# An attention and expert layer on one core: attention passes written out, TensorE order mixed, states as 32x32 diagonal blocks

## What is computed

```python
scores = jnp.einsum('bhid,bhjd->bhij', q, k) * mask      # mask: 0.95**(i-j) for i >= j, else 0
out = jnp.einsum('bhij,bhjd->bhid', scores, v)
out = out.transpose(0, 2, 1, 3).reshape(B, S, D) @ Wo + bo
# group norm of each (batch, head) over its 16 channels and 512 tokens, then gamma and beta
```

## Time and profile before

| | us |
|---|---|
| median of 3 runs | 2576.47 |
| lowest, highest | 2572.44, 2585.91 |
| the profiled execution | 2559.96 |
| its span | 2558.1 |
| PE busy in the span | 2361.7 |
| DVE, ACT, POOL busy | 1349.9, 987.9, 1311.0 |

### The profile page before, as it was taken

How to read it: one execution, slowest core, us unless ns; L and a number is a source line. 1 busy time by engine, 2 the same in 40 slices (tenths; PEclk the granted TensorE clock), 3 DMA queues, 4 the chain that set the end, 5 groups by cost and what they waited for, 6 DMA issues and landing times.

```text
span 2558.1 us, 74894 instructions
## 1 busy us (share of the span) xinstructions
PE 2361.7 (92%) x29260; PEld 2093.5 (82%) x29260; DVE 1349.9 (53%) x2531; ACT 987.9 (39%) x1801; POOL 1311.0 (51%) x2216
## 2 busy tenths in 40 slices
PE   6988888899887899599999999999999999999997
PEld 5777777787766677498999999999999999999996
DVE  2555555566554566595444554445554455544443
ACT  4444444555434454233333333333333333333332
POOL 4333444444333343346666666666666666666453
PEclk9999999999888899699999999999999999999999
DMA  3122222222111211223322323323332323322232
GB/s 118 52 69 72 73 69 76 68 79 75 56 64 51 68 61 60 91 34 49 82 45 46 83 42 49 79 45 49 76 47 46 78 49 64 60 47 45 48 49 25
DMA packets 129237, 155.99 MB, mean 61 GB/s; under 512 B 11008, under 2 KB 118656, under 8 KB 129024
## 3 DMA queue, kind: packets, MB, share of 16 engines
q0 software_dynamic: 49152, 67.14, 16.3%
q1 hardware_dynamic: 79872, 85.58, 10.4%
HBM read 85.57 MB, written 67.11 MB: 60 GB/s over the span
## 4 chain that ended last, share of the span: by engine, by line
PE 56%; POOL 1%; DVE 1%; issue 0%; DMA 0%; ACT 0%; POOLq 0%; DVEq 0%; ACTq 0%
PE hidden L1281 27%; PE y L1296 27%; PE xt L1268 2%; POOL out L1134 0%; POOL xg L1124 0%; DMA out<-y,scatter_idx 0%; DVE best_index L199 0%; DVE g_hi L1248 0%; DVE best L195 0%; DMA xg<-xn_rows,step_idx 0%; DVE g_lo L1250 0%; DVE rows L203 0%; DVE xt_lo L1237 0%; ACT y L1183 0%; ACT g L1197 0%
## 5 line engine op out<-in xcount | busy, mean ns | idle before, releaser
L1134 POOL DMA_INDIRECT out<-y,scatter_idx x256 | 436.8, 1706 | 408.7 <-ACT y L1183 349.2
L1248 DVE CAST g_hi<-g 128x512 fp32r<-128x512 f32 x512 | 281.7, 550 | 673.9 <-ACT g L1197 673.8
L1296 PE MATMUL y<-w_hi,g_hi 128*128 128x256 f32 x2048 | 572.2, 279 | 1.8 <-ACT y L1183 1.8
L1296 PE MATMUL y<-w_lo,g_hi 128*128 128x256 f32 x2048 | 566.6, 277 | 0.0
L1296 PE MATMUL y<-w_hi,g_lo 128*128 128x256 f32 x2048 | 566.5, 277 | 0.0
L1197 ACT ACTIVATE g<-hidden 128x512 f32<-128x512 f32 x512 | 306.6, 599 | 400.5 <-PE hidden L1281 400.5
L1281 PE MATMUL hidden<-xt_hi,w_lo 128*128 128x512 f32 x1024 | 404.4, 395 | 0.0
L1281 PE MATMUL hidden<-xt_lo,w_hi 128*128 128x512 f32 x1024 | 402.2, 393 | 0.0
L1281 PE MATMUL hidden<-xt_hi,w_hi 128*128 128x512 f32 x1024 | 399.0, 390 | 1.5 <-DVE xt_lo L1237 1.5
L1250 DVE TENSOR_TENSOR g_lo<-g,g_hi 128x512 fp32r<-128x512 f32 x512 | 386.0, 754 | 17.7
L1296 PEld LDWEIGHTS y<-w_hi,g_hi 128*128 128x128 f32 x2048 | 384.8, 188 | 2.0 <-ACT y L1183 2.0
(11 more groups left out here) (138 smaller groups left out, 3809.7 us busy)
## 6 DMA issues: line engine op xcount, KB each, us to landing
x<-in_x SPq DMA_DIRECT2D x32, 512.0 KB, 4.8
w_stage<-in_w SPq DMA_DIRECT2D x16, 1024.0 KB, 5.7
xn_rows<-xn SPq DMA_DIRECT2D x32, 512.0 KB, 3.4
res<-in_x SPq DMA_DIRECT2D x32, 512.0 KB, 3.8
out<-res SPq DMA_DIRECT2D x32, 512.0 KB, 3.0
xg<-xn_rows,step_idx POOLq DMA_INDIRECT x256
out<-y,scatter_idx POOLq DMA_INDIRECT x256, 3.9
cst<-in_cst SPq DMA_DIRECT2D x1, 484.0 KB, 4.4
```

What stands on the lines that cost most here:

```text
L1134: pool.indirect_dma_start(out_rows, bass.IndirectOffsetOnAxis(sidx[:, k:k + 1], 0), y[:, k, :], None, compute_op=ALU.add).then_inc(scatter ...
L1248: dve.tensor_copy(g_hi[:, m, :], g32[m % 4][:]).then_inc(gh_ready, 1)
L1296: last = pe.matmul(yb[k % 2][:, 0:D], g_[:, m, cols], w[par][:, m, :], start=i == 0, stop=i == 3 * FT - 1)
```

## The change

1. The two loops of the attention block are gone: `passes` writes out all 35 passes on PE, DVE, ACT, POOL and SP, so all waits have constant values, and `wait_apart` is left out of this block. The loops of the expert block stay.
2. The state stays compact: `states` multiplies the 128x32 blocks with a mask of 32 columns, 448 columns in all where it had 1792. The inter-chunk product is made of four matmuls on 32x32 tiles on the array's diagonal, one for each pair of heads, instead of one on the full array. All four write the same PSUM bank, in different partitions.
3. `values` is cut: `inter` of the first half comes right behind `project`, the products of scores and values are done chunk by chunk (0 to 3), and TensorE's order is mixed anew; `av_done` counts four for each batch.
4. The orders of ACT, DVE and POOL are changed to fit. `rsqrt_steps` takes one step of third order and one of second in place of three of second: 11 chained steps instead of 13 without the eps step (which moved out). POOL's group chain goes from 19 steps to 17.
5. DVE computes the group's moments between the two masks of the first scores, and a whole round of top-k at one place; the softmax steps go to the end of the pass.

```diff
-        def passes(eng, one):
-            for b in range(-2, 2):
-                one(b, b % 2)
-            with eng.Fori(1, MID // 2) as i:
-                one(2 * i, 0)
-                one(2 * i + 1, 1)
...
+        def passes(one):
+            for b in range(-2, B + 1):
                 one(b, b % 2)
...
             def states(f, fp):
...
-                dve.tensor_tensor(tm[fp][:].rearrange("p j h (r x) -> p (j h) r x", r=PAIRS),
-                                  sbk[:, 0, 0:n * 32].rearrange("p (g x) -> p g x", x=32).unsqueeze(2)
-                                  .broadcast_to([P, n, PAIRS, 32]),
...
+                dve.tensor_tensor(tm[fp][:].rearrange("p j h x -> p (j h) x"),
+                                  sbk[:, 0, 0:n * 2 * HD].rearrange("p (g x) -> p g x", x=2 * HD),
+                                  bdm.unsqueeze(1).broadcast_to([P, n, 2 * HD]), ALU.mult).then_inc(tm_ready, 1)
...
+            def inter(b, par, z):
...
                     for h in range(DH):
                         at = h * 256 + c * SUB
-                        pe.matmul(ob[:, s, at:at + SUB], tm[par][:, g - 1, h, :],
-                                  qd[par][:, h, g * SUB:(g + 1) * SUB], start=s not in opened, stop=False,
-                                  skip_group_check=True)
+                        for p in range(PAIRS):
+                            rows = slice(32 * p, 32 * p + 32)
+                            pe.matmul(ob[rows, s, at:at + SUB], tm[par][rows, g - 1, h, :],
+                                      qd[par][rows, h, g * SUB:(g + 1) * SUB], start=g in (1, 2) and h == 0,
+                                      stop=False, skip_group_check=True)
```

More of the change, by code:

```diff
@@ L584, in one @@
                 if has(a):
-                    projected(a, 0)
-                if has(l):
-                    norm(l, par, 0)
-                if has(a):
-                    projected(a, 1)
+                    for h in range(DH):
+                        projected(a, h)
                 if has(f):
@@ L593, in one @@
                 if has(l):
+                    norm(l, par, 0)
+                if has(f):
+                    value(f, 2)
+                if has(l):
                     norm(l, par, 1)
@@ L697, in residual, with softmax, one @@
                                   ALU.add).then_inc(res_ready, 1)
-            def one(b, par, k, group=None):
-                f, fp, a = b + 1, 1 - par, b - 1
-                if has(b + 2):
-                    stats(b + 2, k + 1, par)
-                if isinstance(b, int) and b == -2:
-                    split_weights()
-                if group == 1:
-                    route.as_float(dve, 0)
+            def softmax(b, par):
+                if par and has(b):
+                    for m in range(SOFTMAX_SPLIT):
+                        route.softmax_step(dve, b // 2, m, scored)
+                elif not par and has(b - 1):
+                    for m in range(SOFTMAX_SPLIT, Routing.STEPS):
+                        route.softmax_step(dve, b // 2 - 1, m, scored)
+            def one(b, par):
+                f, fp, a, g = b + 1, 1 - par, b - 1, b - MID
                 if has(a):
@@ L743, in one @@
                         x_split(b + 2, h)
-                if has(f):
-                    states(f, fp)
                 if has(a):
@@ L748, in one @@
                         residual(a, j)
[L749 removed]
+                if has(f):
+                    states(f, fp)
+                if b not in (MID, B):
+                    softmax(b, par)
+                if b == B:
                     for r in range(Routing.LAST_PASS_ROUNDS // 2, Routing.LAST_PASS_ROUNDS):
                         route.whole_round(dve, 1, r)
[L753 to L765 removed]
+            passes(one)
         @block.tensor
@@ L973, in one @@
                         project(b, a, h)
+                if has(b):
+                    inter(b, par, 0)
                 if has(f):
-                    for t in range(TT):
-                        value_gate(b, f, t)
-                if isinstance(b, int) and b == B:
+                    value_gate(b, f, 0)
+                    value_gate(b, f, 1)
+                if b == B:
                     route.turn_top(pe, 0, sbk[:, 0, :])
@@ L995, in one @@
                 if has(f):
-                    running_state(b, f, fp)
-                if has(b):
-                    values(b, par, 1)
-                if has(a):
-                    for j in range(2):
-                        turn_y(b, a, j)
-            passes(pe, one)
+                    running_state(b, f, fp, False)
+                if has(a):
+                    turn_y(b, a, 0)
+                if has(f):
+                    running_state(b, f, fp, True)
+                if has(a):
+                    turn_y(b, a, 1)
+                if has(b):
+                    values(b, par, 3)
+            passes(one)
 def expert_block(nc, xn_d, out, w1, w2, cst, route, s1, w_in, out_stored):
```

287 lines of the change are left out of this document (143 added, 144 removed).

## The result

The changed kernel took 2485.8 us (median of 4 runs, 2482.7 to 2487.6) where the kernel before, on the same chip in the same rounds, took 2574.5: a ratio of 0.9655, with a 95% interval of 0.9609 to 0.9701. That is 3.0 to 3.9% faster. The change's own time hardly moved between two chips (2485.8 and, in the repeat, 2484.9), while that of the kernel before did.

The account below looks back on a forecast made before the run. PE and what stops it bound the attention block. 25.4 work + 3.0 packet stops + 0.2 waits = 28.6 us a pass against 31.25; 82 + 2 us off 2560 gives 2476, plus 16.5 to the median: 2492 us, range 2405 to 2580.

Parts of the forecast that it names:

- The clock: Attention block: mean granted clock 0.93, against 0.99 in the expert block, could add to a no-gain case of chance 0.15.
- Loops: Attention block's loop ends: twelve PE stops of 3.33 us each go, 40 us or 1.3 us a pass.
- The product: Inter-chunk product: 28 instructions of 121 ns become 28 four-tile groups of 66 ns, a gain of 1.5 us a pass.
- DVE's and POOL's savings: Attention block: DVE's 1.5 us saved on states and POOL's two steps fewer in each chain are worth nothing.
- The packets' stops: Dense part of each pass: PE waits for instruction packets, 3.8 us per 256 instructions; 3.0 us a pass taken.
- other idle time: PE's waits between engines in each attention pass: 0.2 us, mostly swallowed by its stops for instruction packets.
- stops of 0.5 to 2 us: Sign of being right: stops without a releaser this long, spread over values and running state, some 90 us in all.
- Packets stop nothing: Attention passes: a packet may be ready at every crossing, 25.6 us a pass, about 2400 us; chance 0.20.
- The packets eat the gain: Attention passes: all 4.2 packets must come and group sums are late, 31.1 us a pass, 2570 us; chance 0.15.
- Serial tiles: Inter-chunk product: diagonal tiles writing one bank run one behind the other, 172 to 352 ns a group, 2584 to 2740; chance 0.12.
- My point of 160 ns: Inter-chunk product: from about this time for a group of four tiles, the changed kernel is slower than before.
- The change doesn't do what it says: Attention block: two or three branches might remain, the 40 us gain would be missing, about 2532 us; chance 0.03.

Follow-up runs that it names:

- the repeat: The unchanged change measured once more, on the chip of the runs with added weight loads: 2484.9 us, ratio 0.9714 to the kernel before.
- the written-out kernel: The kernel before with only its two attention loops written out, same order and full-array product: 2514.5 us against 2559.9, ratio 0.9823.
- The half-packet shift: The change with 32 tiny matmuls ahead of everything on TensorE, moving PE's later code by 128 instructions: 2491.6 us, ratio 0.9749.

## Why the prediction was right

**The total, partly by luck.** 2492 forecast, 2485.8 measured; 28.6 us a pass forecast, 28.94 measured. Misses cancelled. The sum counted 46 us for the diagonal product, which is worth nothing that the runs can tell in this order; it had no term for the mixed order, which gave 29 us beside the full array; and it added 16.5 us from the profiled execution to the median, where the change's are 3.2 apart (2482.65 and 2485.8, against a profiled execution of 2476 by the sum). The clock was a term only in a rival and at nothing in the sum; by the estimate above it is some 22 us of the gain.

**Loops: right.** 40 us forecast, 45 measured alone. By the waits, 32 us of it are stops; the sum had all of it there.

**The product: the size right, the gain not.** 66 ns a group forecast, 64 measured; 1.85 us a pass forecast, 1.8 measured by the starts (0.80 and 1.02) and 1.97 by the durations. But this term cannot be put into the sum by itself. 28 instructions became 112, and the stops grew with them: by 77 us in the old order (a net loss of 49) and by 21 in the new one (nothing left that the runs can tell). I charged the packets once for the whole pass, so the sum came out right while "a gain of 1.5 us a pass" did not: without the diagonal product the time would have been the same (2485.1 us, ratio 0.9709).

**The mixed order: not named as a gain, and the larger part of one.** With the full-array product the change's order and its smaller edits take the written-out kernel from 2514.5 to 2485.1 us, 29 us. With the diagonal product they take it from 2563.8 (ratio 1.0004) to the change's ratio of 0.9655 to 0.9714, some 75 to 90 us. I had a term for each part of the change but this one; it was hidden in the estimate of the stops. The parts of this step (the new order on PE, the orders of DVE and POOL, the shorter Newton chain) were not taken apart. That DVE's and POOL's savings are worth nothing is argued from their cover alone: DVE is busy for 533 of 990 us.

**The packets' stops: 3.0 us a pass forecast, 77.3 us between the group sums measured, 2.5 a pass**, and 0.5 us of other idle time where 0.2 was forecast: the 93.2 us of idle time above are 3.0 a pass. The busy time is 804.1 / 31 = 25.9 us a pass, 25.4 forecast. The sign "stops of 0.5 to 2 us" held for every second pass only; most of the passes between had one of more than 2. The rule of the Trainium skill, "Runtime: NRT & Kernel Launch", section Instruction fetch mechanics, that a block's crossing is mostly hidden, does not hold for this code: written out and without a branch, it stops for 79.6 us. The half-packet shift bears out the block of 256, and the ends of the stops, each 1.2 to 1.6 us behind a packet, bear out the cause.

**The rivals.** *Packets stop nothing* (2400) falls by the 79.6 us. *The packets eat the gain* (2570) is wrong for the change, and is just what the diagonal product does in the old order: ratio 1.0004. *Serial tiles* fall by the 64 ns; ordered to be serial they cost 194 ns a group and give 0.9877, still faster than before, since the stops shrink as the work grows. My point of 160 ns, from which the kernel would be slower, left that out. The rule "TensorEngine Tiling (Array Packing)", Gotcha 1 (PSUM Pressure), of the Trainium skill, that different row tiles cannot access one bank at the same time, is not borne out for four diagonal tiles that write different partitions: 64 ns side by side against 194. *The change doesn't do what it says* falls by the 194 packets and the absence of the 3.3 us stops at every second pass.

**Not tried:** the diagonal product inside the hardware loops.

## What to carry to other kernels

Where small matmuls stand close together, an instruction has a price of its own, in the supply of the queue: a rewrite that gives one matmul four quarters has to be charged for the added packets before its shorter array time is counted. In such code, long matmuls belong between the dense pieces, not at one end of the pass; moving two tiles of six matmuls and one group of transposes gave 0.6 to 1.2% here (by the two ratios of the change), while nearly halving the product's time (3.38 to 1.82 us a pass by the starts) gave nothing. And before adding up a change's terms, ask which of them draw on the same resource: those have to be tried together.

## What the runs showed of the hardware

**A long stop costs twice.** Behind most of the long stops for instructions the transposes of x take 1.97 us in place of 1.09. From the change (first fence, with the clock of the stretches before and behind the stop) and, with a shorter stop, from its repeat (second):

```profile
640.84 0.95 PE L892 MATMUL attn<-s_sb,v_parity 64*32 64x64 f32 x46 [2.51 <-issue]
641.73 1.97 PE L773 MATMUL front<-cst,xn 128*128 128x128 f32 x8
...
634.00:640.80 6.80, 4.34 (x222) 3.52 (x220) 4.53 (x9) 3.26 (x7) 5.86 (x16) 1.00 0.51 155
640.90:644.20 3.30, 3.30 (x62) 2.62 (x66) 0.64 (x1) 1.26 (x3) 0.29 (x1) 0.50 0.03 8
```
```profile
352.27 0.75 PE L892 MATMUL attn<-s_sb,v_parity 64*32 64x64 f32 x52 [2.13 <-issue]
352.95 1.09 PE L773 MATMUL front<-cst,xn 128*128 128x128 f32 x8
```

The granted clock is 1.00 up to the stop's end and 0.50 behind it, the two levels of 2.4 and 1.2 GHz; from 644.3 to 698 us it is 1.00 again. In the change's trace, of the 26 groups of eight that no stop divides, 9 took 1.97 us and one 1.70; nine of these ten stand 0.6 to 1.0 us behind a stop of 2.4 to 3.5 us, one behind 1.86. The other 16 took 1.09 or 1.10, one of them behind a stop of 2.50 and two behind 2.23 and 2.32. For this line alone that is 9 x 0.88 + 0.61 = 8.5 us. By this, two short stops should be better than one long one of the same sum; no run tried that by itself.

**A semaphore increment on TensorE's queue** costs 0.13 to 0.15 us (stops of 8.15 and 9.81 us with 64 in them, if nothing else is in these stops), where one instruction of the diagonal product starts 16 ns after the one before.
